# A graph-network kernel: stage ends without a GpSimd drain, result stores moved to SyncE, first count load in three parts

## What is computed

```python
h = relu(layernorm(x))                                   # 3125 x 256
# layer 0: one message per edge, summed into its first node, then an update of the nodes
m = relu(concat(h[src], h[dst], edge_attr) @ mW1 + mb1) @ mW2 + mb2
agg = segment_sum(m, src)
x = x + h + relu(concat(h, agg) @ uW1 + ub1) @ uW2 + ub2
# layer 1: three graph convolutions over the same edges plus a loop at each node
h = relu(layernorm(x))
norm = rsqrt(deg[src]) * rsqrt(deg[dst])
for W, b in ((W1, b1), (W2, b2), (W3, b3)):              # gelu after the first two
    h = segment_sum((h @ W)[src] * norm, dst) + b
x = x + h                                                # the result, 3125 x 256
```

## Time and profile before

| | us |
|---|---|
| median of 3 runs | 2148.41 |
| the three runs | 2148.41, 2148.63, 2143.78 |
| the profiled execution, its own time | 2150.04 |
| its span (first to last instruction) | 2148.2 |
| stage 1 | 0 to about 566 |
| stage 2 | to 1249 |
| stage 3 | to 1595 |
| stage 4 | to the end |

### The profile page before, as it was taken

How to read it: one execution, slowest core, us unless ns; L and a number is a source line. 1 busy time by engine, 2 the same in 40 slices (tenths; PEclk the granted TensorE clock), 3 DMA queues, 4 the chain that set the end, 5 groups by cost and what they waited for, 6 DMA issues and landing times. The chain is left out here.

```text
span 2148.2 us, 34105 instructions
## 1 busy us (share of the span) xinstructions
PE 1856.5 (86%) x8860; PEld 1252.2 (58%) x8860; DVE 1543.6 (72%) x4318; ACT 795.9 (37%) x1973; POOL 1241.1 (58%) x1461
## 2 busy tenths in 40 slices
PE   3677877775399999999999969998969999999997
PEld 2344454443155555555555536666647788788776
DVE  8877777776299988999988968988877345335332
ACT  0221222221155555555555536655662122113000
POOL 3777777777687777777777739998967000000000
PEclk7676777787699999999999979999999999999999
DMA  5111111111376666666666862212244234343232
GB/s 157 43 55 51 56 56 56 56 56 51 92 199 190 190 191 185 189 190 191 189 188 189 176 187 69 67 63 65 70 119 148 80 114 121 96 120 118 89 118 89
DMA packets 181702, 254.09 MB, mean 118 GB/s; under 512 B 29245, under 2 KB 144762, under 8 KB 181515
## 3 DMA queue, kind: packets, MB, share of 16 engines
q0 software_dynamic: 47888, 126.25, 21.6%
q1 hardware_dynamic: 101186, 99.11, 15.0%
q10 hardware_dynamic: 32440, 26.55, 3.8%
HBM read 202.35 MB, written 49.37 MB: 117 GB/s over the span
## 5 line engine op out<-in xcount | busy, mean ns | idle before, releaser
L971 POOL DMA_INDIRECT brow<-B_rows,rows x440 | 464.8, 1056 | 178.5 <-DVE pre L1074 109.8
L372 POOL DMA_INDIRECT src_list<-ring,ring_row x392 | 400.0, 1021 | 151.5 <-issue 117.6
L1865 PE MATMUL pO<-F,y 128*128 128x512 f32 x1728 | 436.4, 406 | 9.8 <-DVE y L1685 6.6
L1865 PEld LDWEIGHTS pO<-F,y 128*128 128x128 f32 x1728 | 326.8, 190 | 89.0 <-DVE y L1685 6.8
L1002 PE MATMUL pEdge<-A,turned 128*128 x880 | 333.2, 490 | 0.0
L1074 DVE TENSOR_TENSOR pre<-pEdge,brow 128x1024 f32<-128x1024 f32 x220 | 268.7, 1221 | 50.9 <-PE pEdge L1002 42.6
L1230 POOL TENSOR_SCALAR src_oh<-iota,src_s 128x128 bf16<-128x128 bf16 x426 | 281.1, 676 | 31.2 <-PE pC L1401 30.0
L1011 PE MATMUL pNode<-hid_whole,oh 128*128 128x512 f32 x440 | 227.7, 599 | 20.9 <-DVE sums L1092 20.9
L1681 DVE CAST F<-raw 128x512 fp32r<-128x512 uint16 x432 | 173.8, 439 | 66.8 <-PE pO L1865 61.6
L1036 ACT ACTIVATE turned<-pTurn 128x256 fp32r<-128x256 bf16 x220 | 84.8, 386 | 313.3 <-PE pTurn L990 313.3
L1275 DVE TENSOR_SCALAR dst_oh<-iota_cw,dst_s 128x458 bf16<-128x458 f16 x568 | 187.0, 376 | 0.0
(11 more groups left out here) (290 smaller groups left out, 3038.9 us busy)
## 6 DMA issues: line engine op xcount, KB each, us to landing
raw<-C_rows SPq DMA_DIRECT2D x72, 768.0 KB, 4.4
C_rows<-c_rows ACTq DMA_DIRECT2D x175, 114.5 KB, 1.7
rows<-src_list SPq DMA_DIRECT2D x110, 100.0 KB, 2.6
brow<-B_rows,rows POOLq DMA_INDIRECT x440, 3.7
U_parts<-part_u SPq DMA_DIRECT2D x25, 256.0 KB, 2.1
B_rows<-bst SPq DMA_DIRECT2D x25, 256.0 KB, 2.1
src_list<-ring,ring_row POOLq DMA_INDIRECT x392
sums<-U_parts SPq DMA_DIRECT2D x17, 256.0 KB, 5.8
```

Source lines behind the costliest of these rows:

```text
L372: nc.gpsimd.indirect_dma_start(dr.src_list[:, :, :].rearrange("p t w -> (p t) w"), bass.IndirectOffsetOnAxis(ap=ring_row[:, k % RING, t:t ...
L971: nc.gpsimd.indirect_dma_start(brow[:, t % BR, :], None, dr.B, bass.IndirectOffsetOnAxis(ap=rows_i[:, m % LCS, j, 1:2], axis=0)).then_inc( ...
L1865: last = mm(pO[m % 2][half][:, :], y[:, win, part, half * P:(half + 1) * P], F[:, n % FS, :], start=(win == 0 and part == 0), stop=False)
```

## The change

All four blocks are opened with `no_gpsimd_drain=True`, which leaves POOL's Drain out of the block's end and keeps the join by semaphores. In stage 4 the first load of counts, until now one DMA of 6 windows, is three DMAs of 2 windows, each with a semaphore of its own (`first_in`). The widening waits for a part every second window instead of once for the whole. The 25 stores of the result move from the end of ACT's program to the end of SP's, with the same waits, in the same order. Two pairs of semaphores are merged: `raw_tail` counts on `w_in` beside the weights (so `widen_tail` waits for the weights too), and `id_done` and `yr_done` become `picks_done`.

```diff
-        block = stack.enter_context(nc.Block())
+        block = stack.enter_context(nc.Block(no_gpsimd_drain=True))     (in all four stages)
@@ graph_layers
+        FIRST = 2
-        tail_in = g.sem("tail_in")
-        id_done = g.sem("id_done")
+        picks_done = g.sem("picks_done")
+        first_in = [g.sem(f"first_in{n}") for n in range(RAWW // FIRST)]
-        yr_done = g.sem("yr_done")
@@ sync
-                        sp.dma_start(raw[:, n % RAWS, :, :],
-                                     rows[:, m * RAWW:(m + 1) * RAWW, c * CHUNK:(c + 1) * CHUNK]
-                                     ).then_inc(raw_in[n % RAWS], 16)
+                        step = RAWW if n > 0 else FIRST
+                        for j in range(0, RAWW, step):
+                            sp.dma_start(raw[:, n % RAWS, j:j + step, :],
+                                         rows[:, m * RAWW + j:m * RAWW + j + step, c * CHUNK:(c + 1) * CHUNK]
+                                         ).then_inc(first_in[j // step] if n == 0 else raw_in[n % RAWS], 16)
                         if n == RAWS - 1:
-                            sp.dma_start(raw_tail[:, :, :], rows[:, 0:LASTW, CHUNKS * CHUNK:N]).then_inc(tail_in, 16)
+                            sp.dma_start(raw_tail[:, :, :], rows[:, 0:LASTW, CHUNKS * CHUNK:N]).then_inc(w_in, 16)
+            for win in ORDER:
+                sp.wait_ge(sum_used, turn_of(L - 1, win) + 1)
+                n = rows_in(win)
+                sp.dma_start(out[win * P:win * P + n, :], keep.resid[0:n, win, :]).then_inc(stored, 16)
+            sp.wait_ge(stored, 16 * NW)
@@ vector
-                dve.wait_ge(tail_in, 16)
+                dve.wait_ge(w_in, 16 * (L + 1))
-                if n % RAWW == 0:
-                    dve.wait_ge(raw_in[m % RAWS], 16 * (m // RAWS + 1))
+                if n < RAWW:
+                    if n % FIRST == 0:
+                        dve.wait_ge(first_in[n // FIRST], 16)
+                elif n % RAWW == 0:
+                    dve.wait_ge(raw_in[m % RAWS], 16 * (m // RAWS + (m % RAWS > 0)))
@@ scalar
-            for win in ORDER:
-                act.wait_ge(sum_used, turn_of(L - 1, win) + 1)
-                n = rows_in(win)
-                act.dma_start(out[win * P:win * P + n, :], keep.resid[0:n, win, :]).then_inc(stored, 16)
-            act.wait_ge(stored, 16 * NW)
@@ tensor
-                    pe.wait_ge(w_in, 16 * L)
+                    pe.wait_ge(w_in, 16 * (L + 1))
```

More of the change, by code:

```diff
@@ L276, in a_part @@
             return keep.A[:, (2 * w + 2 + k) * HID:(2 * w + 3 + k) * HID]
-        block = stack.enter_context(nc.Block())
+        block = stack.enter_context(nc.Block(no_gpsimd_drain=True))
         @block.sync
@@ L1653, in ids @@
             def ids():
-                dve.wait_ge(id_done, 1)
+                dve.wait_ge(picks_done, 1)
                 v.tensor_tensor(last_id[:, :], pL[:, 0:1], own_id[:, :], ALU.add).then_inc(id_ready, 1)
             def widen_tail():
-                dve.wait_ge(tail_in, 16)
+                dve.wait_ge(w_in, 16 * (L + 1))
                 v.tensor_copy(F_tail[:, :, :], raw_tail[:, :, :]).then_inc(tail_ready, 1)
@@ L1759, in heavy_rows @@
             def heavy_rows(k):
-                act.wait_ge(yr_done, k + 1)
+                act.wait_ge(picks_done, k + 2)
                 nc.scalar.copy(y[P // 2:P, LASTW, :, :].rearrange("p k n -> p (k n)"), pP[P // 2:P, :]
@@ L1841, in heavy_ids @@
                     last = mm(pL[:, 0:2], pick[:, win, :], row_id[:, win, :], start=(win == 0), stop=(win == NW - 1))
-                last.then_inc(id_done, 1)
+                last.then_inc(picks_done, 1)
             def picked(k):
@@ L1851, in picked @@
                               start=(win == 0), stop=(win == NW - 1))
-                last.then_inc(yr_done, 1)
+                last.then_inc(picks_done, 1)
             def tile(k, c, win):
```

## The result

Over six runs of each the changed kernel has a median of 2131.6 us (2127.17 to 2137.03), the kernel before 2147.85; the ratio is 0.9928, 95% interval 0.9908 to 0.9948. The forecast was 2131.4. The interval allows a saving of 11 to 20 us, and four more runs of the same kernel in a later series gave 2128.84 and 0.9916 (0.9894 to 0.9938), so that the median came within 0.2 us of the forecast is luck. The profiled execution took 2128.05 us, of which the span is 2126.2, so its span is 22.0 us shorter than before's, 5 us more than forecast.

The account below looks back on a forecast made before the run. PE was taken as busy for 95% of stage 2 and 98% of the last 448 us, so only time without work could go: 8.0 + 2.05 + 6.95 = 17.0 us, 2148.41 - 17.0 = 2131.4 us, range 2125 to 2140.

Parts of the forecast that it names:

- The Drain: End of stage 1: POOL's Drain is the gap left after the last scatter's landing and the join; omitting it saves 8.0 us.
- The other joins: Later stage borders: leaving out POOL's Drain gains nothing, at most 0.5 us at each of three.
- The stores: End of stage 4: stores issued from SP leave under the last chunk's matmuls, saving 6.95 us.
- The parts: Start of stage 4: with the first load split in three, DVE and PE start 2.05 us sooner.
- I set its last packet at 1599.15 and its landing at 1600.0: Stage 4's first load: the first part, 0.262 MB, lands 2.05 us sooner than the whole load did.
- The cover behind the parts: Stage 4's first chunk: other inputs and later loads are ready in time, with 3.8 us reserve against the 2.05 us gain.
- The picks move with it: Stage 4: POOL's picks start after DVE's ranks, right behind the first `lower`, so they move with the sooner start.
- The upper bound for the split: Stage 4's start: at most 3.7 us sooner, plus up to 2 us if the clock stayed up.
- the gap is not the Drain: Rival, end of stage 1: the gap is not the Drain or moves with it; 2139.4 us, chance 0.13.
- the parts take back what they give: Rival, stage 4's first load: each part pays its own start-up, PE 1.0 us later; 2134.5 us, chance 0.10.
- the gathers pay for the missing Drain: Rival, stage 2: the Drain's work is settled under 440 gathers; at 0.34 us each 2171 us, chance 0.03.

Follow-up runs that it names:

- e1: The kernel before, with POOL's Drain left out at the end of stage 1 alone: 2138.59 us, ratio 0.9968.
- e2: The changed kernel with POOL's Drain put back at the end of stage 1 alone: 2136.78 us, ratio 0.9951.
- e5: The changed kernel with explicit POOL Drains: two behind stage 1's scatter waits, one before the first pick, one right behind the indirect load's issue: 2141.34 us.
- e10: The changed kernel with nine small IOTAs on POOL, then a Drain, behind the scatter waits at stage 1's end: 2137.99 us, one run.
- e3: The kernel before with only the 25 result stores moved from ACT to SP: 2139.8 us, ratio 0.9971.
- e7: The changed kernel with ACT's three bias-row broadcasts issued after its 12th window of `y` instead of at stage 4's start: 2126.9 us, ratio 0.9906.
- e8: The changed kernel with the first load in parts of 1, 2 and 3 windows instead of 2, 2 and 2: 2125.55 us, one run.
- e11: The changed kernel with POOL's 25 additions of b3 spread over the second layer: 2123.24 us, ratio to the kernel before 0.9897.
- e12: The changed kernel with the changes of e11 and e7 together: 2119.1 us, ratio to the kernel before 0.9875.

## Why the prediction was right

**The Drain.** Predicted 8.0, measured 8.09, and e1 and e2, with the Drain put back by hand in e5, show that it is the Drain. Reading the scatter's landing off another waiter of the same instruction was what sized it: the gap that is left is 2.68 us, where 2.8 was forecast. The other joins cost what was forecast, nothing, because DVE covers POOL there. e10 adds what the trace of before couldn't say, that the price begins with the Drain and not with the last scatter; had it run down by itself, the wait for the landing would have hidden 1.4 us of it, and a little work between would have hidden the rest.

**The stores.** Predicted 6.95, measured 7.06 (7.04 alone in e3). The 2.15 us behind DVE's last row are the last store's own.

**The parts.** This is the term of the sum that was mis-sized: 2.05 was forecast, and PE started 1.2 us sooner, which at equal clock is still there at the last window's tile. The step that failed is "I set its last packet at 1599.15 and its landing at 1600.0". SP's queue did move more than the part's 0.262 MB in the first 4 us, 0.34 MB, and yet the part landed 5.31 us after its issue, not 4.46: either those bytes were partly the later parts', or the landing took longer than 0.85 us; the view can't tell the two apart. e7 shows what stood beside it, ACT's three broadcasts on their own queue: without them it lands in 2.94 us. The prediction looked at SP's queue only and never asked what else moves in those 4 us.

**The cover behind the parts.** "The picks move with it" held, and so did the sum's assumption that nothing behind the start takes the gain back: at equal clock the lead of the split, of e7 and of e8 is still there when PE reaches the last pieces of chunk 1. What the prediction didn't ask is how the clock goes there. PE's 36 matmuls ahead of the last window's tile take 8.77 to 11.08 us from one execution to the next, more than this term's whole size. It also passed over what was to be won behind the start: in chunk 1 PE waits for DVE, and DVE is slowed by POOL's additions, 6 us that e11 takes away. The upper bound for the split, 3.7 us of start and 2 us of warm clock, was too generous in both: the clock of the first 4 us stayed at 0.50, though PE started sooner.

**The rivals.** That the gap is not the Drain fell with e1 and e2. That the parts take back what they give fell too: the later parts are in time, and SP's queue moves as much in its first 8 us with them as without. That the gathers pay for the missing Drain fell with 1051 ns per gather after 1056.

**The range** held every run of the changed kernel, 2125.4 to 2137.0, the lowest by 0.4 us. The hit of the median is in part luck: the terms were worth 16.4 us and not 17.0, the kernel before has 2147.85 over six runs and not 2148.41, and the two errors cancel; between two series of the changed kernel the median moves by 2.8. The spread of stages 1 and 3 fills the range, more than the doubt about the terms, which the prediction took from one run of before.

## What to carry to other kernels

A Drain of POOL at a stage's end was paid in full where POOL's 392 scatters were the last work, and was free where another engine ended last; read the landing off any other waiter of the same DMA before pricing it. Before splitting a first load, look at what the other queues issue in the same microseconds: here moving three small broadcasts brought PE's start 2.4 us forward, on top of the split's 1.2. Before a sooner start is called lost, compare the granted clock of the pieces behind it: here one piece of 36 matmuls hides 1.6 to 2.3 us in some executions and nothing in others. Look for the work that slows an engine on the path: 25 additions on POOL that nobody waited for yet cost some 6 us, because they slowed DVE where PE waited for it. The kernel with both moved has the lowest median of all (2119.1 us).

## What the runs showed that I had not expected

- A Drain of POOL has no fixed price: 8.1 us behind 392 scatters that have landed, 0.3 at most behind one indirect load that has, 1.4 with none for over 300 us, and about nothing right behind another Drain. Right behind the issue of an indirect load POOL stood until the load's landing. The 8.1 begin only when the Drain does. What it settles stays open; I tried no smaller number of scatters.
- In stage 4 the same work takes one of two times at two places, and where it is longer the granted clock is down: the picks' 25 products take 5.8 us or 7.4, and the 36 matmuls before the last window's tile 8.77 us or 10.3 to 11.1. The clock is 0.77 instead of 1.00 at the first place, 0.76 to 0.82 at the second, that is, partly at the lower level of 1.2 GHz. It was long at the first place in the first profiled execution of the changed kernel and at the second in its second, at the second in e8, at neither in e2, e10 and e11, at both in e7. In e2 and e10 the clock falls just before the second place too (0.91 over the 19.7 us before the piece), but it is full again when the piece starts; PE was busy for 15.7 and 15.8 of these us there, and for 15.5 in the second execution of the changed kernel, where the piece is long. At the first place a fall is absorbed where PE waits for DVE anyway (the last window's tile at 68.76 us against 68.52 in e2 and 68.34 in e10), at the second it is not (70.20). In e12, where nothing absorbs it, it is what is missing from the gain over e11. What decides it between executions stays open.
